# Eight unread bf16 matmuls per group on TensorE, in a segment-max kernel on one core

## The reference, cut to what matters

```python
x_src, x_dst = x[src], x[dst]
theta_x = (x_dst - x_src) @ theta_w.T + theta_b
phi_x = x_src @ phi_w.T + phi_b
e = relu(theta_x + phi_x)
out = segment_max(e, dst, num_segments=x.shape[0])     # 0 where a node has no edge
return layernorm(x + out)
```

## Time and profile before

| | |
|---|---|
| time, three runs | 1243.34, 1245.99 (median), 1250.09 us |
| profiled execution | 1242.66 us, span 1240.8 us |
| busy in the span | PE 313.0 us, DVE 518.0, ACT 274.6, POOL 807.9 |
| mean granted clock of PE | 0.573 of full speed |
| PE work | 953 matmuls, 953 weight loads |

### The profile page before, as it was taken

The page is one execution under the profiler, slowest core; times in us unless marked ns, Lnnn a source line. Parts: engine busy times, 40 slices in busy tenths (PEclk is TensorE's granted clock), DMA queues, the critical chain, the costliest instruction groups (busy, mean ns, idle before and its releaser), DMA issues.

```text
span 1240.8 us, 5980 instructions
## 1 busy us (share of the span) xinstructions
PE 313.0 (25%) x953; PEld 194.2 (16%) x953; DVE 518.0 (42%) x1191; ACT 274.6 (22%) x568; POOL 807.9 (65%) x840
## 2 busy tenths in 40 slices
PE   6363322444342343110000000100014342430000
PEld 5142111222121232000000000000012131210000
DVE  4002332545343454543333433543325253537698
ACT  2022132233232232321111211321101010100144
POOL 6724756766666766677765676677746667667574
PEclk9667565666566655555555555555557565656555
DMA  8567545666465665676655665776547476747264
GB/s 262 164 196 225 178 156 169 229 204 210 159 204 181 215 213 194 231 241 201 199 191 166 209 192 191 256 228 206 192 139 261 145 236 225 240 136 229 100 195 157
DMA packets 111584, 245.76 MB, mean 198 GB/s; under 512 B 19141, under 2 KB 51226, under 8 KB 111546
## 3 DMA queue, kind: packets, MB, share of 16 engines
q0 software_dynamic: 39984, 109.21, 30.8%
q1 hardware_dynamic: 71130, 135.51, 29.9%
q10 hardware_dynamic: 432, 0.66, 0.2%
HBM read 129.89 MB, written 115.45 MB: 198 GB/s over the span
## 4 chain that ended last, share of the span: by engine, by line
DVE 29%; another core or an unknown queue 27%; issue 19%; POOL 10%; PE 6%; ACT 5%; DMA 4%; DVEq 1%; SPq 0%; ACTq 0%; POOLq 0%
DVE acc L582 16%; POOL rows L315 9%; DVE hist L582 6%; ACT hist L379 3%; DMA rows<-b_table,idx 2%; DVE stats L692 1%; PE acc L411 1%; DVE a_sb L681 1%; DVE hist L689 1%; DVE reached L596 1%; DVE a_sb L676 1%; PE ps_b L427 1%; PE ps_a L411 1%; DVEq L580 1%
## 5 line engine op out<-in xcount | busy, mean ns | idle before, releaser
L315 POOL DMA_INDIRECT rows<-b_table,idx x731 | 701.3, 959 | 372.2 <-issue 208.4
L379 ACT COPY hist<-acc 128x512 f32<-128x512 f32 x253 | 147.3, 587 | 471.0 <-DVE hist L582 241.3
L582 DVE SCALAR_TENSOR_TENSOR acc<-acc,reset,rows 128x256 f32<-128x256 f32 x253 | 124.7, 493 | 116.2 <-DVE acc L582 41.9
L582 DVE SCALAR_TENSOR_TENSOR acc<-hist,reset,rows 128x256 f32<-128x256 f32 x201 | 98.7, 491 | 151.5 <-issue 52.6
L582 DVE SCALAR_TENSOR_TENSOR hist<-acc,reset,rows 128x256 f32<-128x256 f32 x253 | 122.3, 483 | 80.8 <-DVE acc L582 41.0
L427 PE MATMUL ps_b<-diff_sb,conv_t 128*128 128x256 f32 x204 | 93.7, 607 | 223.5 <-issue 119.0
L447 PE MATMUL ps_d<-hi,row_of 128*128 128x512 bf16 x98 | 48.7, 497 | 381.3 <-remote 181.1
L462 PE MATMUL ps_a<-theta_sb,xt_sb 128*128 128x256 f32 x196 | 77.6, 545 | 130.6 <-issue 77.8
L427 PEld LDWEIGHTS ps_b<-diff_sb,conv_t 128*128 128x128 f32 x204 | 54.6, 295 | 243.0 <-issue 144.6
L582 DVE SCALAR_TENSOR_TENSOR acc<-hist,reset,early 128x256 f32<-128x256 f32 x51 | 25.2, 495 | 137.5 <-ACT hist L379 93.2
L384 ACT ACTIVATE signs<-ps_d,node_up 128x782 bf16<-128x782 f32 x49 | 44.7, 912 | 151.6 <-issue 74.6
(11 more groups left out here) (120 smaller groups left out, 342.9 us busy)
## 6 DMA issues: line engine op xcount, KB each, us to landing
runmax<-hist SPq DMA_DIRECT2D x260, 384.0 KB
rows<-b_table,idx POOLq DMA_INDIRECT x731
b_table<-rows SPq DMA_DIRECT2D x7, 896.0 KB
xt_sb<-in_xt SPq DMA_DIRECT2D x49, 128.0 KB
early<-in_x SPq DMA_DIRECT2D x12, 512.0 KB
out<-hist SPq DMA_DIRECT2D x11, 512.0 KB, 2.9
xt_sb<-in_xt SPq DMA_DIRECT2D x7, 512.0 KB
xt_sb<-in_xt SPq DMA_DIRECT2D x7, 384.0 KB
```

What stands on the lines that cost most here:

```text
L315: pool.indirect_dma_start(out=rows[:, PLACE[k], :], out_offset=None, in_=b_table, in_offset=bass.IndirectOffsetOnAxis(ap=idx[:, k:k + 1], ...
L379: nc.scalar.copy(hist[:, slot:slot + n - 1, :], acc[:, at:at + n - 1, :]).then_inc(s_copied, 1)
L582: nc.vector.scalar_tensor_tensor(new, former, reset[:, k:k + 1], row_at(k), ALU.min, ALU.max).then_inc(s_fold, 1)
```

## The change

From group 1 on, PE waits at the end of its part of each group until all folds of the groups before are done (`s_fold` at `START[g]`), and then issues eight matmuls of `cols_b` (128 columns of weights) with 512 columns of `hi`. They write a bank of PSUM that nobody reads at that time and count no semaphore up. That makes 260 times 8, or 2080, matmuls with as many weight loads. Nothing else is changed.

```diff
+WARM = 8
...
                         mm = pe.matmul(ps_a[t % 2][:, 0, :], xt_sb[:, t % (2 * CHUNK), k, :], theta_sb[:, k, :],
                                        start=(k == 0), stop=(k == KC - 1))
                     mm.then_inc(s_amm, 1)
+                if g:
+                    unread = ps_a[0] if g < min(A_AT) else ps_t
+                    pe.wait_ge(s_fold, START[g])
+                    for _ in range(WARM):
+                        pe.matmul(unread[:].rearrange("p j d -> p (j d)"), cols_b[:], hi[:, 0:HALF], start=True, stop=True)
```

## The result

The changed kernel takes 1323.44 us (median; 1313.15 to 1328.71 in four runs), the kernel before 1244.66 us in the same measurement (1240.62 to 1250.09). The ratio of the runs is put at 1.0613, with a 95% interval from 1.0559 to 1.0666 (the two medians divide to 1.063). By the medians the change costs 79 us, not the 250 us that I forecast.

What follows compares the result with a forecast made beforehand. No engine was full; POOL's gathers were nearest to a bound, with pauses for folds delayed by PE's late signals. 1240.8 + 135 + 112 + 2 gave a 1490 us span, forecast as 1495 us; range 1170 to 1945.

Steps and rivals of the forecast that it cites:

- the mechanism that I named: PE over-full and its signals slowed by instruction count, so folds come later; 1370 to 1800 us, chance 0.44.
- Term (1): PE's own time for 2080 matmuls: +135 us at the lower clock, 0 at the higher one.
- Term (2): Unread matmuls ahead of PE's next signal displace folding in fourteen slow stretches, 8 us each: +112 us.
- Term (3): PE's wait for s_fold holds back the next conversion's product and transposes; no price of its own.
- Term (4): At the end, the transposes of the last maxima stand behind the last eight matmuls: +2 us.
- The faster one: Busy PE keeps the higher clock and signals at once, so folds come faster, also between 560 and 925 us; 1180 us, chance 0.20.
- The fixed delay: PE's signals have a fixed delay, so only the unread matmuls' time counts; 1260 to 1380, likeliest 1320 us, chance 0.20.
- Nothing that counts: PE's free time hides all, or stretches shorten by as much as PE's work grows; 1246 us, chance 0.06.
- PE bound by its signals throughout: Slow stretches return at once nearly throughout, +563 us for late signals; 1941 us and more, chance 0.10.

Runs made afterwards that it cites:

- wait_only: The changed kernel with PE's wait kept and no unread matmuls; 1081.58 us against 1081.91 us for the kernel before, ratio 1.0000.
- after_again: The changed kernel unaltered, measured again; 1081.32 us against 1080.79 us for the kernel before, ratio 1.0003.
- narrow8_c: The changed kernel with its eight unread matmuls at 64 columns in place of 512; 1347.36 us against 1273.83 us for the kernel before, ratio 1.0581.

## Why the prediction was right and wrong

**Slower, by the mechanism that I named: right.** The time lies in the range, far below its middle. POOL's waits for folds rose, but to 207 us and not to 250. Long waits for marks appeared between 545 and 1000 us, where none over 4 us had been. Unread matmuls lie 20 us and more ahead of ACT's reading, as forecast. The groups to 101 took 432 us, not 480.

**Term (1), +135 us for PE's own time: wrong, and it is the step that failed.** I took the lower clock, "at which 0.50 to 0.62 of full speed puts all three parts now", though the added work itself fills the gaps in which the clock had fallen (0.545 in wait_only, 0.869 in after_again). The granted clock was 0.82, 0.72 and 0.84, and PE was busy for 279 of 396 us at most, 70%. I had written that at the higher clock the term is 0, and 0 it was, as far as the runs can tell: in narrow8_c an eighth of the columns costs as much, 5.8%. Without the term my sum gives 1360 us, 37 above the measured time. (The 0.21 us of this term were read from matmuls of another form, 67 of float32 with 256 columns; the bf16 ones of 512 columns turned out the same, 0.22 us.) The row of the section "Why this matters for your kernels" in the Trainium skill, "TensorE: Matmul & The Clock Gate", that wants no gaps between bursts speaks of the clock, and the trace agrees with it in that; but the kernel was not faster for it in either condition, since its path doesn't go through PE's speed.

**Term (2), +112 us for late signals: right in kind, too large by half.** Measured are 76 us more in POOL's waits, against 112. Three things in my working were off. I let the stretches stay fourteen and grow by two groups of folding each. In fact two folds in a row started over 9 us apart 16 times before and 36 times after. The marks' stretches filled out to what POOL's slots allow, eleven of thirteen to between 20 and 25 us, in the middle part that I had left aside, and the part with A, which I had counted in, lost only 1 us. An unread matmul cost 1.17 us in the stretch shown above, and not the 2.6 us that I took from float32 matmuls. And something came back: between 560 and 925 us the folds no longer start 1.45 us apart but 0.6 (the middle value is 1.46 before and 0.60 after). The rival had said so, but the clock is not the reason, since in narrow8_c the folds start 0.6 us apart too, in the same stretch of time and at a granted clock of 0.51 there. That this repaid part of the loss is read from the trace and was not tried by itself.

**Term (3), the wait without a price:** 0 in the prompt condition, three times measured; open in the late one, where the 79 us may hold a part of it. **Term (4), +2 us:** 97.2 became 99.4 us, +2.2.

**The rivals.** The faster one fell: the clock rose, half of the late signals did not vanish, and there was no gain. The fixed delay gave almost the time that came, 1320 us, but for the wrong reason: its loss was the unread matmuls' own time, and with an eighth of the columns most of that would have gone; ACT's longest wait for a mark also grew, from 12.4 us to 24.6. That its number fits is luck. "Nothing that counts" is what holds in the prompt condition, though with nothing to cancel: there PE has the room and no signal is late. PE bound by its signals throughout did not come: POOL's 18 slots ended the long stretches, also with sixteen a group.

## What to carry to other kernels

Sometimes one engine's signals reach their readers tens of microseconds after its records say that the work is done. Then price added instructions by their number ahead of the next signal and not by their time, and look for what bounds such a stretch (here the 18 slots of POOL). Do not take a clock from a profile in which the engine idles for a change that fills its idle time. And measure the kernel before beside every experiment: the same program took 1081 or 1245 us, and the same change cost nothing or 6%.

## What the runs showed of the hardware

- PE's end signals come late only in some measurements (kernel before 1081 against 1245 to 1274 us, one chip in both), and there, in the one late trace without gathers in the loop, not at all: with plain loads in the same measurement the longest wait for a mark is 1.5 us. In a slow stretch one or two matmuls start every 1.40 us, the same for 64 and 512 columns.
- In the prompt condition 28 extra matmuls of 64 columns a group cost 0.3%, eight of 512 columns nothing, and sixteen of 512 columns 10.9%.
- Matmuls of 512 columns of bf16, each with a weight load of its own, start 0.22 us apart at the higher clock (16 in 3.61 us, the last of which fills 0.38).
- In the late kernel before DVE waits for its own folds as well, up to 1.5 us at a time and 99 us in all (0.8 us in the changed kernel, 1.0 in wait_only). This has not been explained.
- An indirect DMA of 128 rows occupies POOL for 0.95 us, and 0.30 us lie between two: 731 of them took 918.5 us with no pause.
